# First batch's context maxima from fp32 products with head-masked keys, mask rows written by ScalarE, and a new order of work

## The reference, cut to what matters

```python
x = x + tanh(g_xattn) * attention(layernorm(x), ctx)
x = x + tanh(g_ffn) * experts(layernorm(x))

# attention(x, ctx), per head of 8 channels, scale = 1/sqrt(8)
y  = softmax(causal(q @ k.T * scale)) @ v        # q, k, v from x
y += softmax(qc @ kc.T * scale) @ vc             # qc from x; kc, vc from ctx
return y @ Wp + bp

# experts(x): top 2 of 4 groups, then top 4 of the experts left, weights scaled
out = sum_e combine[:, e] * ((silu(x @ w_gate[e].T) * (x @ w_up[e].T)) @ w_down[e].T)
```

## Time and profile before

| | |
|---|---|
| time, median of 3 runs | 350.06 us (346.69 to 352.23) |
| time of the profiled execution | 343.95 us |
| span in its trace | 342.2 us |
| PE busy | 312.4 us, 91% of the span |
| DVE busy | 265.1 us, 77% |
| ACT busy | 189.9 us, 55% |
| POOL busy | 152.3 us, 45% |
| granted PE clock, mean | 0.97 |

### The profile page before, as it was taken

The page is one execution under the profiler, slowest core; times in us unless marked ns, Lnnn a source line. Parts: engine busy times, 40 slices in busy tenths (PEclk is TensorE's granted clock), DMA queues, the critical chain, the costliest instruction groups (busy, mean ns, idle before and its releaser), DMA issues.

```text
span 342.2 us, 8653 instructions
## 1 busy us (share of the span) xinstructions
PE 312.4 (91%) x3162; PEld 243.9 (71%) x3162; DVE 265.1 (77%) x651; ACT 189.9 (55%) x397; POOL 152.3 (45%) x174
## 2 busy tenths in 40 slices
...
GB/s 125 56 151 134 136 144 115 152 242 159 96 171 106 146 110 155 120 177 95 173 87 159 82 136 143 33 173 147 95 73 105 38 17 81 48 5 138 15 2 15
DMA packets 33847, 37.26 MB, mean 109 GB/s; under 512 B 3726, under 2 KB 31406, under 8 KB 31662
## 3 DMA queue, kind: packets, MB, share of 16 engines
...
## 4 chain that ended last, share of the span: by engine, by line
PE 78%; DVE 8%; DMA 5%; issue 3%; ACTq 2%; SPq 2%; ACT 2%; POOL 0%; DVEq 0%; POOLq 0%
PE bank L952 15%; PE bank L870 14%; PE bank L849 8%; PE bank L977 7%; PE bank L827 7%; PE bank L824 6%; PE bank L846 5%; DVE row_max L1048 3%; PE bank L885 3%; DMA k_stack<-k_scr 2%; DMA q_stack<-shiftT 2%; PE bank L924 2%; PE bank L876 2%; ACTq L460 2%; PE bank L990 1%
## 5 line engine op out<-in xcount | busy, mean ns | idle before, releaser
L1048 DVE TENSOR_REDUCE row_max<-bank 128x2 f32<-128x512 f32 (+1 forms) x224 | 145.7, 685 | 35.9 <-PE bank L824 18.2
L738 ACT ACTIVATE probs<-bank 128x512 f32<-128x512 f32 x224 | 125.6, 597 | 64.3 <-PE bank L849 29.6
L952 PE MATMUL bank<-xn2T,w_pairs_sb 128*128 128x256 f32 x256 | 67.0, 387 | 3.6 <-issue 2.2
L870 PE MATMUL bank<-probs,v_ext 128*32 128x256 f32 (+1 forms) x1024 | 56.8, 363 | 0.0
L649 POOL TENSOR_TENSOR f_h<-f_h,comb 128x512 f32<-128x512 f32 x32 | 40.0, 1274 | 35.8 <-DMA comb<-c_scr 17.1
L952 PEld LDWEIGHTS bank<-xn2T,w_pairs_sb 128*128 128x128 f32 x256 | 43.9, 190 | 10.0 <-issue 3.9
L827 PE MATMUL bank<-k_stack,q_stack 72*128 72x256 bf16 x256 | 46.8, 278 | 1.5 <-DVE row_max L1048 1.1
L849 PE MATMUL bank<-q_stack,k_stack 73*128 73x256 bf16 x256 | 44.4, 276 | 1.4 <-DMA q_stack<-shiftT 1.4
L870 PEld LDWEIGHTS bank<-probs,v_ext 128*32 128x32 f32 x1024 | 29.8, 111 | 19.5 <-issue 3.8
L432 POOL TENSOR_TENSOR rest<-proj,part 128x512 f32<-128x512 f32 x13 | 15.0, 1156 | 50.6 <-ACT part L711 50.6
L824 PE MATMUL bank<-k_stack,q_stack 121*128 121x128 bf16 (+1 forms) x384 | 35.7, 223 | 1.3 <-DVE row_max L1048 0.9
...
## 6 DMA issues: line engine op xcount, KB each, us to landing
...
```

The lines of the kernel that those rows point to most:

```text
L738: nc.scalar.activation(probs[:, seq % NP, :], exp_bank[s % 2][:, :], ACT.Exp).then_inc(exp_done, 1)
L870: last = pe.matmul(pv_bank[32 * n:32 * n + VW, col + q0:col + T], v[:, VW // 2 * odd:VW // 2 * odd + VW], weights, start=odd == 0 and kt = ...
L952: last = pe.matmul(bank_of[:, n * T:(n + 1) * T], w[:, e0:e0 + 128], xn2T[:, :], start=True, stop=True)
L1048: nc.vector.tensor_reduce(row_max[:, kind, h0:h0 + nh, qt], max_bank[k % 2][:, :].rearrange("p (h k) -> p h k", h=nh), AX.X, ALU.max).then ...
```

## The change

Seven things change.

- The 16 context chunks of batch 0 (`first_max_chunk`) are no longer made from the bf16 stacks, but as fp32 products over all 128 channel rows: `first_q` (128x256) against `first_keys[h]`, the keys with all rows but head h's set to zero. q and k come from the projection's bank in two ACT steps (`q32`).
- The 16 masked keys (`hk`) are made one per head, eight on DVE (heads 0 to 7, scalar product with a column of `head_of`) and eight on ACT (heads 8 to 15). They and q, k lie in tiles that the experts and the merge use later (`f_h`, `comb`, `y`, `y_self`).
- DVE makes `head_of`, one reduction of the identity (`heads`).
- Four of the six mask copies (`tri:0:2` to `tri:0:5`, slots 1 and 2) move from DVE to ACT.
- The products of `exp` now wait for batch 0's context stacks, where `max` did.
- `rest` is no tile of its own but lies in `proj`, so the rests are taken in place. Three waits are added for what shares a tile: DVE's first split of batch 0 waits for `q32`, a load of x for the projection, the first spread of the routing weights for the first 16 maxima.
- All five orders are written anew. The loads of the experts' weights (1.5 MB) move on SP from behind batch 2's stacks to the start.

The code, without the table (of which two lines of ACT's order stand):

```diff
     'act': '''
-        xnT_e:0 proj_e:0 fk:0 proj_e:0:1 fk:0:1 fk:0:2 v_e:0 xnT_e:1 fk:0:3 proj_e:1 fk:0:4 fk:0:5 part0:1 v_e:1
-        proj_e:1:1 xnT_e:2 part0:1:1 sh_e:0 exp_e:0 exp_e:0:1 exp_e:0:2 proj_e:2:1 proj_e:2 exp_e:0:3 exp_e:0:4 sh_e:0:2
...
+KEYS_BY = {n: engine for engine in ("dve", "act") for what, b, n in order(engine) if what == "hk"}
...
-        rest = sb("rest", [C, 2, 2 * T])
+        rest = proj
...
+        head_of = sb("head_of", [128, H])
...
+        first_q = y_self[:, :, :].rearrange("p n c -> p (n c)")
+        first_k = y[:, :, :].rearrange("p n c -> p (n c)")
+        first_keys = [(f_h, comb)[h // NB][:, h % NB, :] for h in range(H)]
...
                 if b == 0:
+                    if kind == CROSS:
+                        eng.wait_ge(first_made, 2)
                     first_rest(eng, kind)
...
+            def first_operands():
+                act.wait_ge(proj_ready[CROSS], 1)
+                nc.scalar.activation(first_k, gate_bank[:, T:2 * T], ACT.Identity, bias=cols_sb[:, 3:4]).then_inc(first_made, 1)
+                act.wait_ge(scaled, 2)
+                nc.scalar.activation(first_q, gate_bank[:, 0:T], ACT.Identity, bias=bias_q[:, 1:2]).then_inc(first_made, 1)
+
+            def keys_of_head(h):
+                act.wait_ge(heads_made, 1)
+                act.wait_ge(first_made, 1)
+                nc.scalar.activation(first_keys[h], first_k, ACT.Copy, scale=head_of[:, h:h + 1]).then_inc(keys_by_act, 1)
...
+            def copy_masks(qk, s):
+                act.wait_ge(tri_made, 2)
+                st, tri = ((q_stack, tri_q), (k_stack, tri_k))[qk]
+                nc.scalar.activation(st[64:128, s, SELF], tri[64:128, 0:T].unsqueeze(1).broadcast_to([64, H, T]),
+                                     ACT.Copy).then_inc(masks_in[s], 1)
...
+            def first_max_chunk(k, qt, h0, nh):
+                ge(pe, max_taken, k - 1)
+                if k == 0:
+                    pe.wait_ge(first_made, 2)
+                done = {"dve": 0, "act": 0}
+                for h in range(h0 + nh):
+                    done[KEYS_BY[h]] += 1
+                ge(pe, keys_by_dve, done["dve"])
+                ge(pe, keys_by_act, done["act"])
+                ps = max_bank[k % 2][:, :].rearrange("p (h k) -> p h k", h=nh)
+                for n in range(nh):
+                    last = pe.matmul(ps[:, n, :], first_q[:, qt * 128:(qt + 1) * 128], first_keys[h0 + n], start=True, stop=True)
+                last.then_inc(max_scores, 1)
...
-                if k in (0, CROSS_C1):
+                if k in (0, CROSS_C1) and (b > 0 or kind == SELF):
                     stack_here(pe, b, kind)
+                if b == 0 and kind == CROSS:
+                    first_max_chunk(k, qt, h0, nh)
+                    return
...
                 if b == 0 and s == 0:
                     pe.wait_ge(first_shift_in, 16)
+                    stack_here(pe, 0, CROSS)
...
+            def head_masks():
+                dve.wait_ge(const_made, 1)
+                nc.vector.tensor_reduce(head_of[:, :], ident[:, :].rearrange("p (d h) -> p h d", h=H), AX.X, ALU.add).then_inc(heads_made, 1)
+
+            def keys_of_head(h):
+                dve.wait_ge(heads_made, 1)
+                dve.wait_ge(first_made, 1)
+                nc.vector.tensor_scalar(first_keys[h], first_k, head_of[:, h:h + 1], None, ALU.mult).then_inc(keys_by_dve, 1)
```

More of the change, by code:

```diff
@@ new lines @@
+        down:1:1 max:4:27 xn2T:2 max:5 exp:4:4 down:1:2 logits:2 max:5:1 exp:4:5 exp:4:6 max:5:2 down:1:3 max:5:3
+        exp:4:7 down:1:4 max:5:4 down:1:5 down:1:6 down:1:7 max:5:5 max:5:6 xnT:6 exp:4:8 exp:4:9 pv:4 exp:4:10
+        shift:4:1 exp:4:11 ga:2 up:2 combT:2 max:5:7 exp:4:12 exp:4:13 max:5:8 proj:6 max:5:9 exp:4:14 exp:4:15 ga:2:1
+        y:3:1 max:5:10 exp:4:16 max:5:11 exp:4:17 pv:4:1 max:5:12 exp:4:18 max:5:13 proj:6:1 exp:4:19 max:5:14 max:5:15
+        up:2:1 exp:4:20 yT:3 max:5:16 exp:4:21 ga:2:2 max:5:17 max:5:18 exp:4:22 exp:4:23 shift:5 up:2:2 max:5:19
@@ new lines @@
+        exp:4:24 wp:3 exp:4:25 max:5:20 pv:4:2 max:5:21 exp:4:26 max:5:22 y:4 exp:4:27 exp:5 max:5:23 ga:2:3 exp:5:1
+        max:5:24 exp:5:2 max:5:25 pv:4:3 down:2 exp:5:3 max:5:26 max:5:27 exp:5:4 up:2:3 exp:5:5 exp:5:6 max:6 shift:5:1
+        down:2:1 max:6:1 exp:5:7 max:6:2 exp:5:8 vproj:6 max:6:3 max:6:4 down:2:2 exp:5:9 xn2T:3 max:6:5 down:2:3
+        max:6:6 logits:3 pv:5 xnT:7 down:2:4 max:6:7 exp:5:10 exp:5:11 y:4:1 max:6:8 down:2:5 exp:5:12 exp:5:13 max:6:9
+        proj:7 down:2:6 down:2:7 exp:5:14 max:6:10 up:3 exp:5:15 yT:4 ga:3 max:6:11 max:6:12 combT:3 pv:5:1 max:6:13
@@ new lines @@
+        shift:6:1 max:7:10 exp:6:11 down:3:5 down:3:6 exp:6:12 exp:6:13 y:5:1 down:3:7 max:7:11 exp:6:14 max:7:12
+        exp:6:15 ga:4 exp:6:16 exp:6:17 pv:6:1 combT:4 max:7:13 exp:6:18 exp:6:19 yT:5 up:4 max:7:14 max:7:15 exp:6:20
+        exp:6:21 ga:4:1 y:6 exp:6:22 exp:6:23 up:4:1 wp:5 ga:4:2 max:7:16 max:7:17 pv:6:2 exp:6:24 max:7:18 shift:7
+        up:4:2 exp:6:25 ga:4:3 max:7:19 max:7:20 exp:6:26 exp:6:27 up:4:3 max:7:21 max:7:22 exp:7 exp:7:1 pv:6:3 xn2T:5
+        exp:7:2 down:4 down:4:1 max:7:23 max:7:24 down:4:2 logits:5 exp:7:3 max:7:25 down:4:3 down:4:4 down:4:5 exp:7:4
@@ new lines @@
+        exp:7:5 down:4:6 down:4:7 max:7:26 max:7:27 exp:7:6 exp:7:7 y:6:1 ga:5 exp:7:8 exp:7:9 pv:7 shift:7:1 exp:7:10
+        up:5 combT:5 exp:7:11 exp:7:12 ga:5:1 exp:7:13 yT:6 up:5:1 exp:7:14 exp:7:15 ga:5:2 exp:7:16 wp:6 exp:7:17
+        pv:7:1 exp:7:18 exp:7:19 up:5:2 exp:7:20 exp:7:21 ga:5:3 up:5:3 xn2T:6 exp:7:22 exp:7:23 pv:7:2 y:7 down:5
+        exp:7:24 exp:7:25 logits:6 down:5:1 down:5:2 down:5:3 exp:7:26 exp:7:27 down:5:4 down:5:5 down:5:6 pv:7:3
+        combT:6 down:5:7 y:7:1 ga:6 up:6 yT:7 ga:6:1 wp:7 up:6:1 ga:6:2 up:6:2 ga:6:3 up:6:3 xn2T:7 logits:7 down:6
@@ new lines @@
+    'pool': '''
+        masks:0 rstd1:0 rstd1:1 rows:0 xres:0 xn1:1 xres:1 vclear:0 rstd1:2 vclear:0:1 xn1:2 rstd1:3 sp1:1:1 sp3:1:1
+        xn1:3 sp1:2 sp1:2:1 rstd1:4 sp3:2 sp3:2:1 xn1:4 sp1:3 yadd:0 sp1:3:1 sp3:3 xres:2 rstd2:0 xn2:0 sp3:3:1 yadd:1
+        sp1:4 sp3:4 fhc:0 fhc:0:1 sp1:4:1 fhc:0:2 rstd2:1 sp3:4:1 xn2:1 xres:3 rstd1:5 fhc:0:3 xn1:5 sp1:5 sp3:5 yadd:2
+        sp1:5:1 fhc:1 sp3:5:1 rstd1:6 xres:4 rstd2:2 fhc:1:1 fhc:1:2 xn2:2 fhc:1:3 xn1:6 yadd:3 sp1:6 sp3:6 fhc:2
+        sp1:6:1 sp3:6:1 fhc:2:1 rstd1:7 rstd2:3 xn2:3 xn1:7 fhc:2:2 fhc:2:3 xres:5 yadd:4 sp1:7 sp3:7 sp1:7:1 fhc:3
+        sp3:7:1 rstd2:4 xn2:4 fhc:3:1 fhc:3:2 xres:6 marks:7 fhc:3:3 yadd:5 rstd2:5 fhc:4 xn2:5 fhc:4:1 fhc:4:2 fhc:4:3
+        yadd:6 rstd2:6 xn2:6 xres:7 fhc:5 fhc:5:1 fhc:5:2 fhc:5:3 yadd:7 rstd2:7 fhc:6 fhc:6:1 fhc:6:2 fhc:6:3 fhc:7
```

261 lines of the change are left out of this document (128 added, 133 removed).

## The result

The changed kernel takes 352.38 us (median of 12 runs, 347.05 to 359.2), the kernel before, in the same series, 345.65 us (12 runs, 341.88 to 355.1). The ratio is 1.015, 95% interval 1.0094 to 1.0207: 5.2 us more (0.015 x 345.65), where the forecast had 0.7 more. That the forecast time of 350.8 us lies near 352.38 is luck: it was put on the earlier median of 350.06, 4.4 us above what the kernel before takes here, and the cost of the change was missed by about as much, 4.5 us.

A forecast was written before the change was run, and what follows sets the result against it. PE was taken as the bound, saturated from 60 to 295 us, with only start and tail open. Start +1.7 and tail -1.0 gave +0.7 on 343.95, scaled to 350.8 us; own range 346 to 354, whole range 342.5 to 357.5.

The forecast's parts named there:

- three signs of being wrong: Mask copies under 2 us, the first exponential before 36 us, or the products of L863 0.85 us apart throughout.
- No step that moves there is worth anything: From 60 to 295 us PE is busy 233.87 of 235.00 us, so moved steps there gain nothing unless PE does less.
- The start, +1.7: First 60 us: exponential 17 comes 2.2 us late, less 0.5 us given back by the order; bounds -5 and +9.
- exponential 17: Point in the start where the kernels are compared: ended at 57.0 us before, forecast at 59.2, 2.2 us late.
- The bound of +9: Upper bound of the start's term, from the second rival, in which the fp32 stretch runs at 1.2 GHz.
- the excess of ACT's load: Until exponential 17, ACT gets 18.3 us more with 13.0 left: 5.3 over, about 2.5 after overlap.
- the added 10.1 us of PE work: In the first 60 us, 16 fp32 chunks at 0.86 instead of 0.23 us, covered by 19.2 us of PE idle time.
- the rival at 1.2 GHz: Start: fp32 maxima at half clock take 27.2 us of PE, about +7 us, 351 or 357.5 us; chance 0.14.
- the third rival: Start: POOL holds DVE's eight keys, each losing 0.9 us; +4 more, 348.7 or 354.9 us; chance 0.11.
- The lead over 23.97: Start: the first context maximum comes near 16.5 us instead of 23.97, a lead of 7 us for DVE.
- The lead's survival as a rival: Start: with mask copies at 1.33 us or DMA starts beside them, -6 us with the tail, 344.0 us; chance 0.27.
- The tail, -1.0: Batch 7's output-add for batch 6 moves ahead of three router steps, removing DVE's 1.06 us wait; bounds -2.2 and +0.9.

The follow-up runs named there:

- e10: The changed kernel run once more without an edit, for a second trace: 350.25 us, span 348.5 us.
- e1: The kernel before with the changed kernel's new start up to batch 0's last weighing of values, every engine's old order behind it: ratio 1.0097 to the kernel before.
- e6: The kernel before with its old start, the new order behind batch 0's last weighing, experts' weights loaded behind batch 2's k loads: ratio 0.9977 to the kernel before.
- e7: The changed kernel with SP's old order behind batch 1's first shift row, other engines keeping the new order: ratio 1.0125 to the kernel before.
- e4: The changed kernel with its four mask copies moved back from ACT to DVE: ratio 1.0168 to the kernel before.
- e5: e4 with the first shift row's store moved on SP ahead of three stores of batch 1's parts: ratio 1.0271 to the kernel before.
- the first trace: The first profiled execution of the changed kernel, one of its slower ones: 354.63 us, span 352.8 us.
- e12: Third mended start: fp32 maxima, masks on DVE, start reordered on the engines, old order from batch 0's last weighing on: ratio 1.0260 to the kernel before.

## Why the prediction was right or wrong

The time lies in the forecast's own range, and none of its three signs of being wrong came, but its sum was another: in e10 the start costs 3.0 us instead of 1.7, the middle 5.3 instead of nothing (lateness from batch 0's last weighing to batch 7's), and the tail gives 2.0 back instead of 1.0, together the 6.3 us by which its span is longer.

**"No step that moves there is worth anything": wrong.** This is the step that failed worst. 60 to 295 us read as full, and I took that for robust. I had listed moves on SP in the start alone; `shd:2` behind `qst:3` and `load:5` was a move on a queue that PE waits for, and the busy share said nothing about how little slack the row had. The pair of a late start and that place cost 4 us at one point in both traces of the changed kernel, and did not in e1, e6 and e7; in e4 and e5, which have the pair too, it was 0.7 and 2.2 us there.

**The start, +1.7: sign right, size short, and by the wrong reason.** At the forecast's own point, exponential 17, it is 4.5 us in e10, 4.4 in e1 and 7.3 in the first trace, where 2.2 was forecast; by batch 0's last weighing 3.0, 2.9 and 5.8. The bound of +9 held. ACT's copies were sized exactly (3.6 forecast, 3.62 measured); the Trainium skill's figure (ScalarE: Activation LUTs, What ACT_TABLE_LOAD costs) gave 3.60, and the trace agrees. (Its rule that I named beside it lists relu, max, min, add and mul, not copies; here DVE's copy takes 1.22 us.) But the excess of ACT's load was not what made the start late: e4 takes all of it away and gains nothing. Near 40 to 43 us four things came together, ACT's copies, the row's place on SP, DVE's maxima and PE's list, and taking away one only showed the next. A sum over one engine's load cannot see that.

**The products: sized right.** The chunks of batch 0 in e12, at a clock of 1.00:

```profile
30.95 5.78 PE L873 MATMUL bank<-comb,y_self 128*128 128x256 f32 x24
```

With four records to a chunk these are six chunks, 0.96 us each where 0.86 was forecast. At a clock of 0.50 two chunks took 3.78 us (first trace, from 17.92), 1.9 each where 1.70 was. So the added 10.1 us of PE work was about right, and it was covered as forecast: the sixteenth maximum ends at 40.1 us in the first trace and at 39.6 in e10, in the kernel before at 39.7. The condition of the rival at 1.2 GHz did occur (clock 0.52 from 15 to 22 us in the first trace), for three chunks; from 22 to 40 the clock was 1.00.

**DVE's keys** took 0.55 us each instead of 0.38 (eight in 4.0 us), and the first maximum came at 18.34 instead of 16.5; the third rival's 0.9 us more for each did not come. The lead over 23.97 was real and was used up before the first shift (35.3; forecast about 34), as forecast. The lead's survival as a rival falls with the 3.62 us.

**The tail, -1.0:** not resolved. Both waits named went or shrank; the stretch behind the last weighing is 0.5 to 2.8 us shorter in six traces with the new order there, and longer in two (e5 and e7).

**The clock.** I cited a rule that sustained activity releases the throttle (the Trainium skill, TensorE: Matmul & The Clock Gate, What's actually happening). From 53 to 59.6 us in the first trace PE was busy 6.19 of 6.60 us and the clock was 0.50 there; in the second the window from 53 to 57 shows 0.74. So busy time as the profile counts it did not tell when the clock would rise.
